# Another order for the set-up of a decoder layer kernel: which engine prepares what, and when

## The chip, the cores and the metric

The kernel runs on one core of a Trainium2 chip. A time is the device time of one execution in microseconds. The five engines of the core are TensorE (PE), VectorE (DVE), ScalarE (ACT), GpSimd (POOL) and SyncE (SP). Each runs its own list of instructions in order and waits for the others by semaphores; SP here only issues DMAs, and ACT and POOL issue some too.

## The reference

One decoder layer over x of shape (32, 128, 128): 32 batches of 128 tokens with 128 features. All in float32.

```
x = x + attn(layernorm(x))            # 16 heads of 8, rotary factors on q and k, causal softmax, W_attn, W_proj
x = x + xattn(ctx, ctx, layernorm(x)) # one head of 128, Wq, Wk, Wv, Wo, full softmax over 128 context rows
x = x + ffn(layernorm(x))             # router softmax over 8 experts, the top 2 of them, each silu(x Wg) * (x Wu) Wd,
                                      # plus a shared expert times sigmoid(x gate_w)
```

## The kernel before, in words

**Stages.** A batch is one tile of 128 tokens; four batches are a group (`GB`), eight groups in all. The kernel has a set-up, a loop over the 32 batches for both attentions and the router, then the passage to the experts and the expert part. The change lies in the set-up and in the first steps of the loop.

**Set-up.** SP and ACT issue the loads. PE turns W_attn, W_proj, Wo and the router weights (`transpose` against an identity), multiplies Wk with Wq and Wv with Wo so that each is one matrix later, spreads the rotary table over 128 rows and adds up two bias rows (L626 to L646). All of this goes to four shared PSUM banks, and DVE copies it to SBUF (L1108 to L1124). Before that DVE takes the statistics of the first group of x (L1084, L1089) and arranges the bias rows (`brow`, L1100). POOL writes constants, the causal masks and then normalises group 0 (L529, L531) and clears the value buffer (L561).

**First steps.** For a group, PE turns the normalised x (`turn_x`, L652), and projects keys and queries (`project`, L661: two matmuls of 512 columns); DVE adds the bias and multiplies with the rotary factors (L1146); DMAs put the heads into block form in `k_heads` and `q_heads` (L469), which must be zero elsewhere: that is what the clears of `wide` are for (L1096, 2048 columns each, one for each of keys and queries of two groups). For a batch, `project_v` (L668) makes the values, ACT drains them (L944), `scores` (L678) and a mask (L685) fill four PSUM banks, DVE takes row maxima (L1167), two of them by way of a copy by ACT (L951), `turn_max` (L694) turns them, ACT keeps them, a DMA spreads them (L475), and `scores_t` (L703 to L712) computes the transposed scores less the maxima, of which ACT takes the exponential (L955).

**Order.** Each engine's list in the loop comes from the table `ORDER`: entry (stage, offset, part, which) puts a stage of batch s + offset in slot s. The table is the same in both programs. On PE it yields `turn_x(0)`, `project(0)`, values 0 and 1, `scores(0)`, values 2, `turn_x(1)`, `turn_max(0)`, `scores(1)`, `scores_t(0)`, values 3, `project(1)`, and so on.

```
def late_setup():                      # DVE, L1128: ends_acc, kcol, ramp32, split of the shared expert's gate/up weights
setup_done                             # DVE tells it after the last copy (L1126); PE's project(0) and POOL's bias wait for it
```

## Time and profile before

| | us |
|---|---|
| median of 3 runs | 478.93 |
| lowest, highest | 478.83, 479.94 |
| profiled execution: its own time | 475.0 |
| profiled execution: span | 473.1 |
| PE busy | 427.4 (90%) |
| DVE busy | 358.2 (76%) |
| ACT busy | 293.0 (62%) |
| POOL busy | 203.5 (43%) |

The profiled execution is one of its own; its time stands beside the runs' and not among them. The span is what its instructions cover. Busy times are sums over the whole span and do not say who waits for whom at the start; the chain of waits and the timelines do. Names in the rows: `ps_scores` are the four PSUM banks of the scores, `ps_shared` the four others, `wide` the memory of `k_heads` and `q_heads`, `probs` also holds the raw weights during set-up. A row with xN merges N like instructions; a float32 matmul counts as two. The line numbers are those of the kernel before.

### The profile page before, as it was taken

To read this page: it belongs to the slowest core of one execution; us is meant where nothing else is said; L and a number is where in the kernel's file an instruction comes from. 1 tells how busy PE (TensorE), PEld (TensorE's weight loads), DVE (VectorE), ACT (ScalarE), POOL (GpSimd) and SP (SyncE) were. 2 spreads that over 40 slices of the span, in tenths; PEclk is the share of its full clock that TensorE was granted. 3 is DMA by queue.
4 is the path that set the end of the run, shared out by engine and by line. 5 is a ranking of instruction groups with operands and counts; after the bars stand their busy time and mean duration, and the time that the engine had idled before them with its cause. 6 is when DMAs were issued, how large, how long until landed. Compare 5 with 4: busy or idle time off the path is not lost.

```text
span 473.1 us, 13582 instructions
## 1 busy us (share of the span) xinstructions
PE 427.4 (90%) x4444; PEld 289.8 (61%) x4444; DVE 358.2 (76%) x1232; ACT 293.0 (62%) x951; POOL 203.5 (43%) x247
## 2 busy tenths in 40 slices
PE   4869799999999999999999988769899999999992
PEld 3424455555655655656555555547688888888782
DVE  5474567879889888888797786779577777777595
ACT  1124678887877877878779877463355555555430
POOL 7802012030343262353324235567166666676490
PEclk9999999999999999999999999559999999999998
DMA  7700000101111111011111003512233333232394
GB/s 191 198 24 26 19 19 31 37 10 35 49 29 50 48 48 49 26 54 47 33 47 53 25 28 110 169 51 76 67 100 98 92 93 92 81 104 62 110 318 135
DMA packets 41604, 34.69 MB, mean 73 GB/s; under 512 B 6464, under 2 KB 36432, under 8 KB 41536
## 3 DMA queue, kind: packets, MB, share of 16 engines
q1 hardware_dynamic: 36478, 24.51, 18.4%
q0 software_dynamic: 4320, 8.99, 5.6%
q8 instruction: 37, 0.61, 0.6%
q10 hardware_dynamic: 738, 0.33, 0.3%
q14 instruction: 31, 0.25, 0.2%
HBM read 17.26 MB, written 12.09 MB: 62 GB/s over the span
## 4 chain that ended last, share of the span: by engine, by line
PE 71%; DVE 12%; issue 6%; ACT 4%; POOL 3%; DMA 2%; SPq 1%; DVEq 0%; ACTq 0%; POOLq 0%
PE ps_scores L860 10%; PE ps_scores L678 7%; PE ps_shared L877 7%; PE ps_shared L725 6%; PE ps_scores L707 6%; PE ps_shared L661 3%; PE ps_shared L868 3%; PE ps_scores L703 3%; PE ps_shared L776 3%; ACT probs L955 2%; PE ps_scores L712 2%; POOL xs L593 2%; PE ps_shared L782 2%; PE ps_shared L787 2%; PE ps_scores L852 2%
## 5 line engine op out<-in xcount | busy, mean ns | idle before, releaser
L611 POOL DMA_INDIRECT ys<-ctx_t,xload x71 | 69.1, 974 | 45.2 <-ACT ctx_t L1052 42.7
L955 ACT ACTIVATE probs<-ps_scores 128x512 f32<-128x512 f32 x128 | 69.8, 608 | 17.9 <-PE ps_scores L712 17.9
L599 POOL TENSOR_TENSOR x1b<-x,bias 128x128 f32<-128x128 f32 x32 | 14.4, 451 | 151.0 <-DVE x L1188 151.0
L593 POOL DMA_INDIRECT xs<-xrow,posu x64 | 66.5, 1039 | 26.3 <-issue 13.2
L860 PE MATMUL ps_scores<-wide,xe 128*128 x213 | 66.9, 422 | 0.0
L951 ACT ACTIVATE s_copy<-ps_scores 128x512 f32<-128x512 f32 x64 | 38.4, 604 | 18.7 <-PE ps_scores L685 18.5
L1372 DVE COPY probs<-ps_shared 128x256 f32<-128x256 f32 x71 | 30.2, 425 | 22.8 <-PE ps_shared L868 22.8
L1167 DVE TENSOR_REDUCE negmax<-ps_scores 128x4 f32<-128x512 f32 x64 | 41.1, 684 | 7.4 <-PE ps_scores L685 6.9
L877 PE MATMUL ps_shared<-wd,probs 128*128 x284 | 43.4, 275 | 0.1
L678 PE MATMUL ps_scores<-wide,qk 32*128 32x512 f32 x256 | 38.4, 671 | 3.3 <-ACT probs L955 3.1
L1042 ACT ACTIVATE xe<-ps_scores 128x128 fp32r<-128x128 f32 x71 | 19.7, 278 | 33.8 <-PE ps_scores L852 33.8
L1167 DVE TENSOR_REDUCE negmax<-s_copy 128x4 f32<-128x512 f32 x64 | 40.0, 667 | 0.0
L1047 ACT ACTIVATE vst<-ps_scores 128x256 f32<-128x256 f32 x71 | 27.3, 384 | 18.6 <-PE ps_scores L860 18.6
L877 PEld LDWEIGHTS ps_shared<-wd,probs 128*128 128x128 f32 x284 | 37.2, 191 | 0.3 <-issue 0.3
L860 PEld LDWEIGHTS ps_scores<-wide,xe 128*128 128x128 f32 x213 | 34.8, 190 | 3.0
L725 PE MATMUL ps_shared<-probs,vst 128*32 128x128 f32 x1024 | 34.6, 276 | 0.0
L707 PE MATMUL ps_scores<-wide,qk 32*128 32x512 f32 x256 | 34.0, 601 | 0.0
L1366 DVE SCALAR_TENSOR_TENSOR vst<-vst,xload,ps_scores 128x256 f32<-128x256 f32 x71 | 33.5, 472 | 0.7 <-ACT vst L1047 0.6
L725 PEld LDWEIGHTS ps_shared<-probs,vst 128*32 128x32 f32 x1024 | 26.0, 109 | 5.3 <-issue 4.7
L868 PE MATMUL ps_shared<-ident,vst 128*128 128x128 f32 x142 | 27.2, 273 | 0.6 <-DVE vst L1366 0.5
L868 PEld LDWEIGHTS ps_shared<-ident,vst 128*128 128x128 f32 x142 | 19.5, 140 | 11.1 <-DVE vst L1366 2.1
L1361 DVE TENSOR_TENSOR xe<-ps_scores,xe 128x128 fp32r<-128x128 f32 x71 | 20.7, 292 | 5.0 <-ACT xe L1042 1.5
(220 smaller groups left out, 1012.1 us busy)
## 6 DMA issues: line engine op xcount, KB each, us to landing
xload<-xs SPq DMA_DIRECT2D x71, 66.0 KB, 1.9
wide<-qk SPq DMA_DIRECT2D x64, 64.0 KB, 1.9
wide<-ys SPq DMA_DIRECT2D x8, 512.0 KB, 7.4
ctx_t<-in_ctx SPq DMA_DIRECT2D x32, 64.0 KB, 2.0
out_x<-res SPq DMA_DIRECT2D x8, 256.0 KB, 3.4
ys<-ctx_t,xload POOLq DMA_INDIRECT x71, 2.3
wd<-in_L_ffn_w_down SPq DMA_DIRECT2D x8, 128.0 KB, 3.4
xs<-xrow,posu POOLq DMA_INDIRECT x64, 2.4
```

Source lines behind the costliest of these rows:

```text
L593: pool.indirect_dma_start(out=xs, out_offset=bass.IndirectOffsetOnAxis(ap=posu[:, g % 2, k, u:u + 1], axis=0), in_=xrow[:, g % 2, k, u, :] ...
L611: pool.indirect_dma_start(out=ys, out_offset=bass.IndirectOffsetOnAxis(ap=xload_i[:, i % XL, C + 1:C + 2], axis=0), in_=ybuf[:, i % 4, :], ...
L678: pe.matmul(bank[j][:], qk[r, g % 2, 0, ts], k_heads[r, g % 2, :, ts], start=True, stop=True)
L707: pe.matmul(bank[j][:], qk[r, g % 2, 1, ts], q_heads[r, g % 2, :, ts], start=False, stop=True)
L725: mm = pe.matmul(bank[VW * i:VW * (i + 1), half * T:(half + 1) * T], v_pairs[:, b % 4, pair, r * VH:r * VH + VW], probs[:, b % 2, 2 * pair ...
L860: mm = pe.matmul(PS[i % 2][:], a[:, i % 4, :], m[:, bass.ds(e, 1), :].rearrange("p a f -> p (a f)"), start=(r == 0), stop=(r == 2))
L868: mm = pe.transpose(PM[2 + i % 2][:, f * 128:(f + 1) * 128], xh[:, i % 3, f * 128:(f + 1) * 128], ident[:])
L877: mm = pe.matmul(PM[i % 2][:, 0:C], xhT[:, i % 3, f * 128:(f + 1) * 128], wd[:, bass.ds(e, 1), f, :].rearrange("p a c -> p (a c)"), start= ...
L951: act.activation(s_copy[:, j - 2, :], SC[score_bank(("scores", b), j)][:], ACT.Copy).then_inc(copied, 1)
L955: act.activation(probs[:, b % 2, j * HJ:(j + 1) * HJ, :].rearrange("p a t -> p (a t)"), SC[score_bank(("scores_t", b), j)][:], ACT.Exp)\
L1167: dve.reduce_max(negmax[:, b % 2, j * HJ:(j + 1) * HJ], part.rearrange("p (i t) -> p i t", i=HJ), axis=AX.X, negate=True).then_inc(maxed, 1)
L1366: dve.scalar_tensor_tensor(out=xh[:, i % 3, :], in0=xsilu[:, i % 3, :], scalar=xload[:, i % XL, C:C + 1], in1=PS[i % 2][:, FF:2 * FF], op0 ...
```

## The change

- **Loads.** SP asks for W_attn, the q/k bias row and the rotary table right behind the first group of x, under a semaphore of their own (`first_in`), then for group 1 of x, the small bias columns and rows, and the rest of x. Context and shared-expert loads come behind the query heads of group 0, and the nine loads of the down weights go into the loop, one with each `turn_x2`. Two of the four DMAs that place group 0's keys are issued by ACT.
- **PE** turns W_attn and makes rotary rows and q/k bias in two score banks; the other weights are turned behind `project(0)`, multiplied behind `scores(0)`, and the bias rows are made behind `scores(1)`.
- **ACT** loads its activation table before it issues its weight loads, and drains the weights that DVE drained.
- **DVE** clears `k_heads` of group 0 first, normalises group 0 row by row, and runs `late_setup` at group 1's `turn_x` entry instead of group 0's.
- **POOL** clears `q_heads` of group 0 and both buffers of group 1, normalises from group 1 on, and adds the attention bias to groups 0 and 1 together, when the bias rows are there.

```diff
+            sp.dma_start(wa, W_attn.rearrange("(k p) c -> p k c", p=128)).then_inc(first_in, 16)
+            sp.dma_start(rows[:, 2:4, :], b_attn[0:2 * C].rearrange("(a k n) -> a k n", a=1, k=2)).then_inc(first_in, 16)
+            sp.dma_start(rope4[:], rope[0:HD // 2]).then_inc(first_in, 16)
+            sp.dma_start(res[:, GB:2 * GB, :], x[GB:2 * GB].rearrange("b t c -> t b c")).then_inc(x_in[1], 16)
...
+                if b < NE:
+                    sp.dma_start(wd[:, b, :, :], (w_down[b] if b < E else sw_down).rearrange("(k p) c -> p k c", p=128))\
+                        .then_inc(wd_in, 16)
...
-                for i in range(HJ):
+                for i in range(HJ // 2 if g == 0 and n == 0 else HJ):
                     sp.dma_start(heads[i:128:HJ, g % 2, i, :], qk[i:128:HJ, g % 2, 1 - n, :]).then_inc(placed[g % 2], 16)
+                if g == 0 and n == 1:
+                    for u in range(4):
+                        sp.dma_start(ctx_t[:, u, :], ctx_in[u]).then_inc(ctx_loaded[u], 16)
+                    for k, m in enumerate((sw_gate, sw_up)):
+                        sp.dma_start(wgs_raw[:, k * FF:(k + 1) * FF], m).then_inc(wgs_in, 16)
...
+            pool.memset(q_heads[:, 0], 0.0).then_inc(heads_cleared[0][1], 1)
...
-            norm_x_rows(0)
             const(pool.memset(vst[:], 0.0))
             const(pool.memset(v_parts[:, :, 0:3:2, HD:HD + 1], 1.0))
             assert consts[0] == CONSTS + STORES
             pool.memset(one_row4[:].bitcast(fp32), 1.0).then_inc(ones_set, 1)
             pool.wait_ge(ones_set, 1)
+            norm_x_rows(1)
+            pool.memset(k_heads[:, 1], 0.0).then_inc(heads_cleared[1][0], 1)
+            pool.memset(q_heads[:, 1], 0.0).then_inc(heads_cleared[1][1], 1)
...
+                if g > 1:
                     norm_x_rows(g)
+                w.ge(x_normed, g + 1)
+                if g == 1:
+                    pool.wait_ge(set_drained[3], 2)
+                    add_bias(0)
+                add_bias(g)
...
+            pe.wait_ge(first_in, 16 * FIRST_LOADS)
 
             for k in range(3):
...
+                mm = pe.transpose(SC[0][:, k * C:(k + 1) * C], wa[:, k, :], ident[:])
+            mm.then_inc(set_filled[0], 1)
             pe.wait_ge(arranged, 2)
+            pe.matmul(SC[1][:, 0:2 * C], rope_rows[:], rope4[:].rearrange("p k t -> p (k t)"), start=True, stop=True)
             for k in range(2):
...
+                mm = pe.matmul(SC[1][:, 2 * C + k:2 * C + k + 1], brow[:, k, :], one_row[:, 0:1], start=True, stop=True)
             mm.then_inc(set_filled[1], 1)
 
...
+            def turned_weights():
+                pe.wait_ge(w_in, 16 * W_LOADS)
+                pe.transpose(PM[1][:, 0:C], wsq[:, 4, :], ident[:])
+                pe.transpose(PM[1][:, C:2 * C], wsq[:, 0, :], ident[:])
+                pe.transpose(PM[1][:, 2 * C:2 * C + NE], wr[:], ident[0:NE, 0:NE])
+                pe.matmul(PM[1][:, 3 * C:3 * C + 1], wsq[:, 1, :], cols[:, 2:3], start=True, stop=True).then_inc(set_filled[2], 1)
+
+            def folded_weights():
+                pe.wait_ge(set_drained[2], 1)
+                pe.matmul(PM[3][:, 0:C], wsq[:, 3, :], wsq[:, 1, :], start=True, stop=True)
+                pe.matmul(PM[3][:, C:2 * C], wsq[:, 2, :], woT[:], start=True, stop=True).then_inc(set_filled[3], 1)
+
+            def folded_biases():
+                pe.wait_ge(arranged, 3)
+                pe.matmul(PM[3][:, 2 * C:3 * C], bcol[:, 0, :], wpT[:], start=True, stop=False)
+                pe.matmul(PM[3][:, 2 * C:3 * C], one_row[:], rows[:, 0, :], start=False, stop=True)
+                pe.matmul(PM[3][:, 3 * C:4 * C], bcol[:, 1, :], woT[:], start=True, stop=False)
+                pe.matmul(PM[3][:, 3 * C:4 * C], one_row[:], rows[:, 1, :], start=False, stop=True).then_inc(set_filled[3], 1)
...
+                    if g == 0:
+                        pe.wait_ge(rows_normed, u + 1)
...
+                if g == 0 and n == 1:
+                    turned_weights()
...
+                if b == 0:
+                    folded_weights()
+                if b == 1:
+                    folded_biases()
...
+            act.preload_act_table_set("natural_log_exp_and_others")
             for n, m in enumerate((W_proj, Wo, Wq, Wk, Wv)):
...
+                    first_weights()
+                if g == 1:
+                    first_keys()
+                    turned_weights()
+
+            def first_weights():
+                act.wait_ge(set_filled[0], 1)
+                for k in range(2):
+                    act.activation(wqk[:, k, :].rearrange("p (r d i) -> p r d i", r=NJ, i=HJ),
+                                   SC[0][:, k * C:(k + 1) * C].rearrange("p (r i d) -> p r d i", r=NJ, i=HJ), ACT.Copy)
+                act.activation(wvT[:], SC[0][:, 2 * C:3 * C], ACT.Copy).then_inc(set_drained[0], 1)
+
+            def first_keys():
+                w.bank_read(("project", 0, 0))
+                act.wait_ge(heads_cleared[0][0], 1)
+                for i in range(HJ // 2, HJ):
+                    act.dma_start(k_heads[i:128:HJ, 0, i, :], qk[i:128:HJ, 0, 1, :]).then_inc(k_placed[0], 16)
+
+            def turned_weights():
+                act.wait_ge(set_filled[2], 1)
+                act.activation(woT[:], PM[1][:, 0:C], ACT.Copy)
+                act.activation(wpT[:], PM[1][:, C:2 * C], ACT.Copy)
+                act.activation(wrT[:], PM[1][:, 2 * C:2 * C + NE], ACT.Copy)
+                act.activation(bqA[:], PM[1][:, 3 * C:3 * C + 1], ACT.Copy, scale=XSCALE).then_inc(set_drained[2], 1)
+
+            def folded_weights():
+                act.wait_ge(set_filled[3], 1)
+                act.activation(wA[:], PM[3][:, 0:C], ACT.Copy, scale=XSCALE)
+                act.activation(wM[:], PM[3][:, C:2 * C], ACT.Copy).then_inc(set_drained[3], 1)
+
+            def folded_biases():
+                act.wait_ge(set_filled[3], 2)
+                act.activation(bias1[:], PM[3][:, 2 * C:3 * C], ACT.Copy)
+                act.activation(bias2[:], PM[3][:, 3 * C:4 * C], ACT.Copy).then_inc(set_drained[3], 1)
...
+            dve.memset(k_heads[:, 0], 0.0).then_inc(heads_cleared[0][0], 1)
             dve.wait_ge(const_ready, FIRST_CONSTS)
...
+            group_stats(0)
+            dve.wait_ge(first_in, 16 * FIRST_LOADS)
+            dve.tensor_copy(brow[:].rearrange("a k (r d i) -> a k r d i", r=NJ, i=HJ),
+                            rows[:, 2:4, :].rearrange("a k (r i d) -> a k r d i", r=NJ, i=HJ)).then_inc(arranged, 1)
+            dve.wait_ge(x_rstd, 1)
+            for u in range(GB):
+                dve.tensor_scalar(xn1[:, u, :], res[:, u, :], mv1[:, u, 0:1], rs1[:, u:u + 1], ALU.subtract, ALU.mult)\
+                    .then_inc(rows_normed, 1)
+            dve.wait_ge(rows_normed, GB)
+            dve.memset(rsum[:], 0.0).then_inc(x_normed, 1)
             dve.wait_ge(set_filled[1], 1)
...
+            dve.tensor_copy(ropes[:].rearrange("p k t -> p (k t)"), SC[1][:, 0:2 * C])
+            dve.tensor_copy(bqk[:], SC[1][:, 2 * C:2 * C + 2]).then_inc(set_drained[1], 1)
+            dve.wait_ge(w_in, 16 * W_LOADS)
+            dve.tensor_copy(bcol, cols[:, 0:2].rearrange("p (k a) -> p k a", a=1).broadcast_to([C, 2, C])).then_inc(arranged, 1)
...
             def turn_x(g):
-                if g == 0:
-                    clear(q_heads[:, 0])
-                    clear(k_heads[:, 1])
-                    clear(q_heads[:, 1])
+                if g == 1:
                     late_setup()
```

How instructions move, as the order of each engine's list shows it. First PE, from the bias matmuls of the set-up to the first values and scores; before (L652 turns x, L661 projects, L668 makes values):

```order
L632 MATMUL ps_shared<-one_row,brow 128x1 x2
L635 MATMUL ps_shared<-probs 128x128
L636 MATMUL ps_shared<-cols,probs 128x1
L637 MATMUL ps_shared<-rope,rope_rows 128x256
L642 MATMUL ps_shared<-woT,probs 128x128
L643 MATMUL ps_shared<-wpT,probs 128x128
L644 MATMUL ps_shared<-rows,one_row 128x128
L645 MATMUL ps_shared<-woT,probs 128x128
L646 MATMUL ps_shared<-rows,one_row 128x128
L652 MATMUL ps_shared<-ident,xn 128x128 x4
L661 MATMUL ps_shared<-xT,wqk 128x512 x2
L668 MATMUL ps_shared<-wvT,xT 128x128 x2
```

And now (L666 turns x, L675 projects, L642 to L645 turn weights, L682 makes values, L695 the first scores):

```order
L632 MATMUL ps_scores<-ident,probs 128x128 x3
L635 MATMUL ps_scores<-rope,rope_rows 128x256
L637 MATMUL ps_scores<-one_row,brow 128x1 x2
L666 MATMUL ps_shared<-ident,xn 128x128 x4
L675 MATMUL ps_shared<-xT,wqk 128x512 x2
L642 MATMUL ps_shared<-ident,probs 128x128
L643 MATMUL ps_shared<-ident,probs 128x128
L644 MATMUL ps_shared<-ident,wr 128x9
L645 MATMUL ps_shared<-cols,probs 128x1
L682 MATMUL ps_shared<-wvT,xT 128x128 x2
L695 MATMUL ps_scores<-wide,qk 128x512 x4
```

The weight products and bias rows, six matmuls, no longer stand ahead of the turn of x; three weight turns and a one-column matmul stand between projection and values.

DVE, from the q/k evictions of group 0 to the first row maxima (`negmax`); before:

```order
L1146 SCALAR_TENSOR_TENSOR qk<-ps_shared,bqk,ropes 128x512 x2
L1096 MEMSET wide 128x2048 x3
L1130 MEMSET ends_acc 128x48
L1131 CAST kcol<-ids 128x1
L1132 CAST ramp<-ramps 128x32
L1134 CAST wgs_hi<-probs 128x512
L1135 TENSOR_TENSOR wgs_lo<-probs,wgs_hi 128x512
L1167 TENSOR_REDUCE negmax<-ps_scores 128x4 x2
L1167 TENSOR_REDUCE negmax<-s_copy 128x4 x2
```

And now, from the copy of the bias columns on (L1191 is the q/k eviction, L1209 the row maxima):

```order
L1170 COPY probs<-cols 128x256
L1142 BN_STATS st<-res 128x6 x4
L1147 BN_AGGR mv<-st 128x2 x4
L1191 SCALAR_TENSOR_TENSOR qk<-ps_shared,bqk,ropes 128x512 x2
L1209 TENSOR_REDUCE negmax<-ps_scores 128x4 x2
L1209 TENSOR_REDUCE negmax<-s_copy 128x4 x2
L1142 BN_STATS st<-res 128x6 x4
L1147 BN_AGGR mv<-st 128x2 x4
L1209 TENSOR_REDUCE negmax<-ps_scores 128x4 x2
L1209 TENSOR_REDUCE negmax<-s_copy 128x4 x2
```

Three clears and the late set-up have left the place between the q/k evictions and the first row maxima; the statistics of group 1 stand ahead of the evictions now.

PE, from the mask matmuls of `scores(1)` to `scores_t(0)` (L703 and L707; now L724 and L728); before:

```order
L685 MATMUL ps_scores<-causal,ident 32x512
L685 MATMUL ps_scores<-causal,ident 32x4x96
L685 MATMUL ps_scores<-causal,ident 32x4x64
L685 MATMUL ps_scores<-causal,ident 32x4x32
L703 MATMUL ps_scores<-max_row,one_row 128x512 x4
L707 MATMUL ps_scores<-wide,qk 128x512 x4
```

And now:

```order
L702 MATMUL ps_scores<-causal,ident 32x512
L702 MATMUL ps_scores<-causal,ident 32x4x96
L702 MATMUL ps_scores<-causal,ident 32x4x64
L702 MATMUL ps_scores<-causal,ident 32x4x32
L654 MATMUL ps_shared<-wpT,probs 128x128
L655 MATMUL ps_shared<-rows,one_row 128x128
L656 MATMUL ps_shared<-woT,probs 128x128
L657 MATMUL ps_shared<-rows,one_row 128x128
L724 MATMUL ps_scores<-max_row,one_row 128x512 x4
L728 MATMUL ps_scores<-wide,qk 128x512 x4
```

Four matmuls of the bias rows have come in between; two weight products came in the same way behind `scores(0)`.

## Rows read from the trace of the kernel before

**Rows 1.** the page, its first line, part 4 (chain) and one row of part 6 (DMA)

```profile
span 473.1 us, 13582 instructions
...
PE 71%; DVE 12%; issue 6%; ACT 4%; POOL 3%; DMA 2%; SPq 1%; DVEq 0%; ACTq 0%; POOLq 0%
...
wide<-qk SPq DMA_DIRECT2D x64, 64.0 KB, 1.9
```

**Rows 2.** chain of waits, 15 to 45 us: start, length, what

```profile
16.78 3.77 PE ps_shared L661 x4
...
25.98 1.76 DVE wide L1096
...
28.88 2.48 DVE negmax L1167 x4
...
31.50 0.37 PE ps_shared L694
```

**Rows 3.** ten-microsecond windows: busy time (count) of each engine, PE clock, DMA

```profile
30.00:40.00 10.00, 7.09 (x56) 2.73 (x57) 4.98 (x15) 2.40 (x6) 0.00 (x0) 1.00 0.01 2
```

**Rows 4.** timeline of DVE: start, length, what, [idle before]

```profile
3.83 0.87 DVE L1084 BATCH_NORM_STATS2 st<-res 128x6 f32<-128x128 f32 x4 [3.83 <-DMA res<-in_x]
4.74 0.38 DVE L1089 BATCH_NORM_AGGREGATE mv<-st 128x2 f32<-128x6 f32 x4
...
7.01 0.72 DVE L1100 COPY brow<-rows 1x256 f32<-1x256 f32 x1
...
18.86 0.75 DVE L1146 SCALAR_TENSOR_TENSOR qk<-ps_shared,bqk,ropes 128x512 f32<-128x512 f32 x1 [1.74 <-PE ps_shared L661]
```

**Rows 5.** timeline of PE

```profile
6.79 0.87 PE L626 MATMUL ps_shared<-ident,probs 128*128 128x128 f32 x3 [6.79 <-POOL causal L557]
...
8.40 1.01 PE L632 MATMUL ps_shared<-one_row,brow 1*128 1x1 f32 x4
...
10.29 1.21 PE L637 MATMUL ps_shared<-rope,rope_rows 4*128 4x256 f32 x2
...
12.20 0.64 PE L643 MATMUL ps_shared<-wpT,probs 128*128 128x128 f32 x2
...
14.93 1.11 PE L652 MATMUL ps_shared<-ident,xn 128*128 128x128 f32 x4
16.78 3.75 PE L661 MATMUL ps_shared<-xT,wqk 128*128 128x512 f32 x4 [0.73 <-ACT xT L937]
...
22.54 0.79 PE L668 MATMUL ps_shared<-wvT,xT 128*128 128x128 f32 x2 [0.37 <-ACT vst L944]
23.40 2.09 PE L678 MATMUL ps_scores<-wide,qk 32*128 32x512 f32 x8
...
25.99 0.80 PE L668 MATMUL ps_shared<-wvT,xT 128*128 128x128 f32 x2
27.51 1.12 PE L652 MATMUL ps_shared<-ident,xn 128*128 128x128 f32 x4 [0.72 <-ACT vst L944]
...
31.80 2.09 PE L678 MATMUL ps_scores<-wide,qk 32*128 32x512 f32 x8
...
35.87 0.80 PE L703 MATMUL ps_scores<-max_row,one_row 1*128 1x512 f32 x4 [1.41 <-DVE negmax L1167]
...
39.48 2.09 PE L661 MATMUL ps_shared<-xT,wqk 128*128 128x512 f32 x4
```

**Rows 6.** timeline of DVE, in the loop

```profile
56.15 0.35 DVE L1198 TENSOR_SCALAR xn<-x,mv,rs 128x128 f32<-128x128 f32 x1 [1.02 <-ACT rs L973]
```

**Rows 7.** timeline of ACT

```profile
4.07 1.28 ACT L918 ACT_TABLE_LOAD   x1 [4.07 <-issue]
...
22.21 0.28 ACT L944 ACTIVATE vst<-ps_shared 128x128 f32<-128x128 f32 x1 [4.51 <-PE ps_shared L668]
```

**Rows 8.** timeline of POOL

```profile
13.87 0.21 POOL L562 MEMSET vst<- 128x64 f32 x1
```

**Rows 9.** timeline of the SP queue

```profile
11.85 4.02 SPq L448 DMA_DIRECT2D wd<-in_L_ffn_w_down  x8
```

More of the change, by code:

```diff
@@ L390, in bank_free @@
                 bank, first, width = SLOT[slot]
[L391 to L392 removed]
+                if n == 0 and bank in LATE_SETS:
+                    self.ge(set_drained[bank], LATE_SETS[bank])
                 self.ge(drained[slot], n)
```

111 lines of the change are left out of this document (28 added, 83 removed).

## The prediction

> **What bounds the kernel now.** I read four views, in this order. The page first [rows 1]: TensorE (PE) holds 71% of the chain that ended last, DVE 12%, everything else little. This change does not touch the main loop's work, so what counts is how early the loop gets under way. Next the chain of waits over 15 to 45 us [rows 2]: PE projects keys and queries, and then the chain leaves PE for DVE: three clears of the head buffers and the small late set-up, and only at 28.88 us the first row maxima, with PE's first turn of the maxima at 31.50. Then a window [rows 3]: PE is busy 7.09 of 10 us in 30 to 40. Last the timelines of DVE, PE, ACT, POOL and the SP queue [rows 4 to 9], for durations and spacings. My anchor is PE's first `scores_t(0)` matmul, at 35.87 us [rows 5]: everything that the change inserts or moves on PE lies ahead of it, and from there on both programs run the same instructions on PE in the same order.
>
> **The sum.** I follow the new path, with spacings of the old rows.
>
> Start. The first group of x lands at 3.83, its statistics end at 4.74+0.38 = 5.12 [rows 4]. The new program asks for W_attn, the q/k bias row and the rotary table right behind x, so I take them as landed by then. `brow` costs 0.72 [rows 4]: 5.84. PE, in program order, must do the rotary matmul (1.21) and the two bias matmuls (1.01) before it may turn x [rows 5]: 8.06. DVE's own normalising hides here: four 128x128 rows at 0.35 each, 1.4 [rows 6], behind ACT's rstd. ACT now loads its table (1.28, [rows 7]) ahead of its seven weight loads instead of behind; the statistics wait for either, so the order costs nothing unless ACT is free only after 8.06-1.4 = 6.7. From the first turn of x to the first projection it was 16.78-14.93 = 1.85 [rows 5]: projection at 9.91 instead of 16.78.
>
> To the first scores. The pair of projections takes 3.75: 13.66. Behind it PE now has three weight turns and a one-column matmul: 0.87, and half of 1.01: 15.03. ACT drains them in four copies, about 0.28 each as a like ACT row [rows 7]: 16.15. This wait is new, and behind it on ACT stands the drain of values 0, for which PE waits before values 1. From that drain to PE's next matmul was 22.54-22.21 = 0.33, and from there to the scores 0.86 [rows 5, 7]: `scores(0)` at 17.34 instead of 23.40. Two other inputs come earlier: the keys (DVE reads the projection 2.08 after it starts, 0.75 long [rows 4], then about 0.6 of issue on each of two queues and the 1.9 to landing of [rows 1], 15.3), and POOL's clear of the value buffer (14.08 [rows 8], less the two normalising operations now on DVE, plus one clear of 1.8 that came in: about 13.8).
>
> To the second scores. Scores and causal mask take 25.99-23.40 = 2.59: 19.93. The two weight products inserted here take half of the 2.73 that four such matmuls took (12.20 to 14.93): 21.30. Values 2 and its drain, 0.80+0.33: 22.43. Turning group 1, 1.12, and the maxima, 0.37 [rows 2, 5]: `scores(1)` at 23.92 instead of 31.80. DVE is no longer the one waited for: with the clears gone to POOL its row maxima start when the scores are there, about 19.7, and last 2.48 [rows 2], to 22.2.
>
> To the anchor. Scores and mask again 2.59: 26.51; the four bias matmuls inserted here 2.73: 29.24. In the old program PE waited 1.41 for DVE at this very place [rows 5], so about half of these matmuls is free and half is a loss. `scores_t(0)` comes at 29.2 instead of 35.87: **6.7 us earlier**, all of it at the slow pace of PE. In these sums I used whole durations where neighbours overlap slightly, and left x landing at its old time although ACT's loads no longer crowd it; I put 0.3 us back for that.
>
> **The clock.** The rows of PE run at two speeds. The two projections of group 0 take 3.75, the same pair of group 1 takes 2.09 [rows 5]; the slow ones go with the level of 1.2 GHz, the fast with 2.4, and the column of the granted clock, 1.00 in both [rows 3], does not show it. The change of level fell near 39.7 us, with PE without a gap since 35.87. A first stretch as free of gaps, 6.79 to 16.0, had not brought it. In the new program the gap of 1.41 is filled, so the stretch starts with `scores(1)` or before. If the rise comes as long into it as it did, PE is fast from about 27.5: the rest of the bias matmuls saves 0.7, and `scores_t(0)` with values 3, 39.48-35.87 = 3.61, shrinks in the ratio of 2.09 to 3.75 to 2.0: together 2.3. If it comes only behind `scores_t(0)`, as before, it saves nothing. I take 1.0. Total 6.7+0.3+1.0 = 8.0.
>
> On this the Trainium skill ("TensorE: Matmul & The Clock Gate", section "What's actually happening") says that the throttled state is the default and that activity releases it. By that alone the first stretch should have released it; this trace has it slow at 16.78, and the measurement decides. The rule would let the clock rise with the first scores already; that is a rival below, priced from rows.
>
> The skill ("ScalarE: Activation LUTs", "What ACT_TABLE_LOAD costs") adds a drain of about 1.38 us to each table load. Ahead of the weight loads that would hold all seven back; here the next ACTIVATE starts with the load's end, so I leave it out. With it, the answer would be some 0.7 later.
>
> **What I cost at nothing.** The nine loads of the down weights leave the front of the SP queue and are issued one per batch in the loop, 4.02/8 = 0.50 each [rows 9], where SP waits for the batch anyway. The late set-up (some 1.14: from the end of the last clear, 25.98+1.76, to 28.88 [rows 2]) moves behind group 1's place in the loop, where DVE stood idle 1.02 us for ACT [rows 6]. POOL's two further clears, 1.8 each, end by about 20, and keys of group 1 are wanted only behind its projection, some 8 us before 39.48 [rows 5]. The bias is added to two groups at once, 2.5 us of POOL behind 29.8, wanted only for batch 0's attention output, whose normalised row DVE made at 56.15 [rows 6]. Without that cover the loop pays the first two: at most 9 x 0.50 + 1.14 = 5.6.
>
> **The time.** The profiled execution has a span of 473.1 and a time of 475.0; less 8.0 it is 467.0. The median of the runs is 478.93, 3.9 above it; the difference lies around the span and in the run, and I carry it over: **470.9 us**.
>
> **Rivals.**
> 1. The clock rises early, during or just after `scores(0)`. For: PE's work from there on is dense. Against: the first stretch. `scores_t(0)` then waits for DVE again, as in the old program, where it began 35.87-31.80 = 4.07 after `scores(1)`: 23.92+4.07 = 28.0, 1.25 under the sum; behind it the 1.6 are saved, and some 0.4 on the turns ahead: 3.2. Gain 6.7+0.3+3.2 = 10.2: 468.7.
> 2. The work taken out of the set-up is paid in the loop: a down-weight load stands in front of the heads or the row maxima on SP, and the late set-up pushes row maxima. For: exactly these transfers gate `scores_t`. Against: SP's idle time. Half of 5.6 is paid, and the clock gives nothing: 478.93-7.0+2.8 = 474.7.
> 3. Slower: the clock comes late. PE's order is now another, with more small matmuls; if the change of level misses the stretch around `scores_t(0)`, everything behind stays slow, and each microsecond of work there costs one more. It decides when the slow stage lasts 8 us of fast work (16 us) beyond 29: a rise later than 45 us. A rise at 50 gives about 481. Against: in the old program the loop's density brought it at the first go.
> 4. The change does nothing for the loop: something unseen, a landing of W_attn or a constant of POOL, holds the first projection where it was. Only the DVE clears would then pay, and the bias matmuls eat them: within 1.4 us of 478.9.
>
> **Chances.** Forecast (469.5 to 472.5) 0.50; rival 1 0.20; rival 2 and lesser losses 0.21; rival 3 0.05; rival 4 0.04. Below 0.3% (1.4 us) a change can't be told from none. Faster 0.91, same 0.04, slower 0.05. The range runs from 467.2 (rival 1, and x landing earlier by some 0.6, and 0.9 for what the phase of the clock does at the passage to the experts) to 476.0 (rival 2 with most of its price).
>
> **What would show it.** Right: first projection near 9.9, `scores(0)` near 17, `scores(1)` near 24, `scores_t(0)` near 29 us; row maxima released by PE and not by the end of DVE's clears; bias matmuls directly ahead of `scores_t(0)`. The clock: whether the 3.61 of `scores_t(0)` with values 3 have become 2.0. Wrong: `scores(0)` after 19 (then a wait for POOL, the keys or ACT names itself); a step between two batches above the old one in the first nine batches (rival 2); slow matmuls after 45 us (rival 3).

## The result

The changed kernel takes 465.46 us (median of 4 runs, 464.1 to 467.28), the kernel before 478.88 us beside it: a ratio of 0.9729, 95% interval 0.9704 to 0.9755. It is 13.4 us faster; 8.0 were forecast, and the time lies below the range's low end of 467.2. The profiled execution, one of the four, took 466.55 us, with a span of 464.4, where that of before took 475.0 with 473.1. Of the runs below, one of `clears_back_keep` (496.82 us) and one of `fill_dip` (526.09) were slow executions, over 1.5% above the fastest of the same kernel, and count in no ratio and no median.

The page of the changed kernel, its first line and lines of its parts 1, 2 and 4, answers [rows 1] (here and below, lines that lie between those shown are left out):

```profile
span 464.4 us, 13583 instructions
PE 422.3 (91%) x4444; PEld 287.7 (62%) x4444; DVE 352.8 (76%) x1222; ACT 294.6 (63%) x962; POOL 209.3 (45%) x248
PEclk9998999999999999999999999588899999999997
PE 75%; DVE 9%; issue 6%; ACT 4%; POOL 3%; DMA 1%; SPq 1%; DVEq 0%; ACTq 0%; POOLq 0%
```

PE's share of the last chain rose from 71% to 75%, DVE's fell from 12% to 9%: PE waits less for DVE. PE's timeline of the first 38 us answers [rows 5] (columns: start, us, engine, line, operation, idle time before and its releaser):

```profile
5.05 0.87 PE L632 MATMUL ps_scores<-ident,probs 128*128 128x128 f32 x3 [5.05 <-DMA rope<-in_rotary]
7.65 1.12 PE L666 MATMUL ps_shared<-ident,xn 128*128 128x128 f32 x4
9.45 3.78 PE L675 MATMUL ps_shared<-xT,wqk 128*128 128x512 f32 x4 [0.69 <-ACT xT L993]
13.03 0.42 PE L642 MATMUL ps_shared<-ident,probs 128*128 128x128 f32 x1
14.24 0.77 PE L682 MATMUL ps_shared<-wvT,xT 128*128 128x128 f32 x2
15.38 0.79 PE L682 MATMUL ps_shared<-wvT,xT 128*128 128x128 f32 x2 [0.37 <-ACT vst L1000]
16.10 2.09 PE L695 MATMUL ps_scores<-wide,qk 32*128 32x512 f32 x8
18.70 0.53 PE L649 MATMUL ps_shared<-probs 128*128 128x128 f32 x2
21.41 0.27 PE L715 MATMUL ps_shared<-ident,negmax 128*16 128x128 f32 x1 [0.20 <-DVE negmax L1209]
21.61 1.14 PE L695 MATMUL ps_scores<-wide,qk 32*128 32x512 f32 x8
23.04 0.49 PE L654 MATMUL ps_shared<-wpT,probs 128*128 128x128 f32 x2
24.52 0.50 PE L724 MATMUL ps_scores<-max_row,one_row 1*128 1x512 f32 x4
28.71 1.14 PE L695 MATMUL ps_scores<-wide,qk 32*128 32x512 f32 x8
35.63 1.91 PE L695 MATMUL ps_scores<-wide,qk 32*128 32x512 f32 x8 [1.54 <-ACT probs L1013]
```

`scores(0)` (L695 at 16.10) still takes 2.09, the slow pace; `scores(1)` at 21.61 takes 1.14. So the level rose from 1.2 to 2.4 GHz near 18.9 (two float32 matmuls of 128 columns take 0.53 at 18.70, between the slow 0.80 and the fast 0.49), where it rose near 39.7 in the profile of before. `scores_t(0)`, the anchor (L724), starts at 24.52 instead of 35.87. `scores(3)` at 35.63 is slow again behind an idle 1.54; the window 35 to 40 has a granted clock of 0.66, that of before had 1.00. (The column does not show the slow stretch up to 18.9: it stands at 1.00 there.) DVE, answering [rows 2, 4]:

```profile
5.13 0.49 DVE L1158 COPY brow<-rows 1x256 f32<-1x256 f32 x1
5.82 1.61 DVE L1162 TENSOR_SCALAR xn<-res,mv,rs 128x128 f32<-128x128 f32 x4 [0.20 <-ACT rs L952]
18.79 1.29 DVE L1209 TENSOR_REDUCE negmax<-ps_scores 128x4 f32<-128x512 f32 x2 [4.77 <-PE ps_scores L702]
```

Its row maxima now wait 4.77 us for PE, not for its own clears. ACT drains the turned weights in four short copies from 14.41, then the values at 15.05, as forecast; its seven weight loads issue from 0.85 to 4.23 beside the table load of 0.82 to 2.10. Read one after another, PE's milestones give the whole account:

| start on PE, us | before | forecast | after | ahead |
|---|---|---|---|---|
| first projection | 16.78 | 9.91 | 9.45 | 7.33 |
| `scores(0)` | 23.40 | 17.34 | 16.10 | 7.30 |
| `scores(1)` | 31.80 | 23.92 | 21.61 | 10.19 |
| `scores_t(0)` | 35.87 | 29.2 | 24.52 | 11.35 |
| `scores(2)` | 41.77 | | 28.71 | 13.06 |
| `scores(4)` | 55.65 | | 43.86 | 11.79 |
| `scores(31)` | 272.78 | | 260.98 | 11.80 |
| end of the span | 473.1 | | 464.4 | 8.7 |

From `scores(4)` to `scores(31)` the two programs keep the same step to 0.02 us. The loads of the down weights and the late set-up, moved into this loop, cost nothing. Three things are to be explained: why the lead of the loop is 11.8 and not 8.0, why 3.1 of it is gone at the end of the span, and why the medians differ by 13.4 all the same.

### The profile page after: what moved, and what is told of

Same layout as the page of the kernel before. It is cut to its first block, busy times and chain, and to the rows that moved or that the text cites. A ratio compares the mean times of both kernels' runs of the same rounds, so it can differ in the third digit from the quotient of the medians.

```text
span 464.4 us, 13583 instructions
## 1 busy us (share of the span) xinstructions
PE 422.3 (91%) x4444; PEld 287.7 (62%) x4444; DVE 352.8 (76%) x1222; ACT 294.6 (63%) x962; POOL 209.3 (45%) x248
## 4 chain that ended last, share of the span: by engine, by line
PE 75%; DVE 9%; issue 6%; ACT 4%; POOL 3%; DMA 1%; SPq 1%; DVEq 0%; ACTq 0%; POOLq 0%
PE ps_scores L881 11%; PE ps_scores L695 8%; PE ps_shared L898 7%; PE ps_shared L746 7%; PE ps_scores L728 6%; PE ps_shared L675 4%; PE ps_shared L889 3%; PE ps_scores L724 3%; PE ps_shared L797 3%; POOL xs L599 3%; ACT probs L1013 2%; PE ps_scores L733 2%; PE ps_shared L803 2%; PE ps_shared L808 2%; PE ps_scores L873 2%
## 5 line engine op out<-in xcount | busy, mean ns | idle before, releaser
L599 POOL DMA_INDIRECT xs<-xrow,posu x64 | 68.5, 1070 | 25.7 <-issue 13.5
L881 PE MATMUL ps_scores<-wide,xe 128*128 x213 | 68.8, 433 | 0.0
L1209 DVE TENSOR_REDUCE negmax<-ps_scores 128x4 f32<-128x512 f32 x64 | 41.1, 684 | 11.8 <-PE ps_scores L702 11.2
L695 PE MATMUL ps_scores<-wide,qk 32*128 32x512 f32 x256 | 38.2, 668 | 3.2 <-ACT probs L1013 3.1
L1209 DVE TENSOR_REDUCE negmax<-s_copy 128x4 f32<-128x512 f32 x64 | 40.0, 666 | 0.0
L881 PEld LDWEIGHTS ps_scores<-wide,xe 128*128 128x128 f32 x213 | 35.9, 196 | 3.4 <-issue 0.2
L728 PE MATMUL ps_scores<-wide,qk 32*128 32x512 f32 x256 | 33.1, 586 | 0.0
```

Of the source, the lines that this page charges most:

```text
L599: pool.indirect_dma_start(out=xs, out_offset=bass.IndirectOffsetOnAxis(ap=posu[:, g % 2, k, u:u + 1], axis=0), in_=xrow[:, g % 2, k, u, :] ...
L695: pe.matmul(bank[j][:], qk[r, g % 2, 0, ts], k_heads[r, g % 2, :, ts], start=True, stop=True)
L728: pe.matmul(bank[j][:], qk[r, g % 2, 1, ts], q_heads[r, g % 2, :, ts], start=False, stop=True)
L881: mm = pe.matmul(PS[i % 2][:], a[:, i % 4, :], m[:, bass.ds(e, 1), :].rearrange("p a f -> p (a f)"), start=(r == 0), stop=(r == 2))
L1209: dve.reduce_max(negmax[:, b % 2, j * HJ:(j + 1) * HJ], part.rearrange("p (i t) -> p i t", i=HJ), axis=AX.X, negate=True).then_inc(maxed, 1)
```

## The experiments

The runs were on four chips. On one of them before takes 479 us as here (`after_third`, `fill_dip`, `warm_dip`, `clears_only`), on the three others about 500, so each time is compared only with runs of before on its own chip. The four profiles of before, of which three are from chips at 500, reach `scores(4)` at 55.65 to 56.67 us, so milestones of the first 60 us may be set side by side to about 1 us. My theory was that the mechanism is as forecast and the clock term too small. The milestones below are starts of `scores(b)`.

**The same kernels again.** They show how far executions of one program differ.

> The changed kernel once more, unchanged. My theory: the loop's start is fixed by waits and comes again to 0.1 us (scores of batch 2 at 28.7, the last scores at 261, 11.8 earlier than in the old profile), and the 3 us that single executions differ by arise in one place, the passage from the loop to the experts (270 to 330 us), and in where TensorE's clock changes level. Rival: the executions differ already at the start of the loop by a us or more, so that 11.8 is itself a matter of luck. Time 464 to 467.

> The kernel before once more, unchanged. Its profiled execution (475.0) was 3.9 under the median of its runs. My theory: that execution was a lucky one in the passage to the experts or in the clock at the start, and a second profile has the last scores at 272.8 again but a span of 474 to 477. Rival: 3.9 is a constant between a profiled execution and the others; then this profile gives 475.0 again while its runs stay at 479.

> The changed kernel again, for comparison on the same chip. Both theories: 0.972 to 0.980 of the time of the kernel before, scores(0) near 16.2 us, a slow scores(3) and a step of 8.2 us to scores(4), where the other batches take 6.95.

`before_again`: ratio 1.0018 (0.9994 to 1.0042). `after_again`: 0.9791 (0.9749 to 0.9833). `after_third`: 0.9709 (0.9672 to 0.9747), 464.4 us, just under the expected 0.972 to 0.980. The expected clock did not hold, nor did "to 0.1 us": `after_again` has `scores(2)` at 27.70 and not 28.7, `scores(4)` at 42.84, which is 13.6 ahead of `before_again` on the same chip. The profile of `before_again` took 504.49, 1.4 over the median of its runs, so 3.9 under it is not a constant of profiled executions. It has on PE:

```profile
23.47 1.14 PE L678 MATMUL ps_scores<-wide,qk 32*128 32x512 f32 x8 [0.69 <-DMA wide<-qk]
31.57 0.37 PE L694 MATMUL ps_shared<-ident,negmax 128*16 128x128 f32 x1 [4.49 <-DVE negmax L1167]
31.87 2.09 PE L678 MATMUL ps_scores<-wide,qk 32*128 32x512 f32 x8
```

The old kernel too can be fast at `scores(0)`; it then falls back in the wait of 4.49 behind DVE's clears. The same fall shows in `before_third`, and in `before_fourth`, which is fast from 26.8 on: in all three the granted clock is 0.50 in the window 35 to 40. The profile from which I predicted, slow all the way to 39.7, was the exception of four. `after_third` on PE:

```profile
12.23 1.06 PE L675 MATMUL ps_shared<-xT,wqk 128*128 128x512 f32 x1
13.09 0.34 PE L642 MATMUL ps_shared<-ident,probs 128*128 128x128 f32 x1
15.41 1.14 PE L695 MATMUL ps_scores<-wide,qk 32*128 32x512 f32 x8
33.78 1.14 PE L695 MATMUL ps_scores<-wide,qk 32*128 32x512 f32 x8 [1.54 <-ACT probs L1013]
```

Here the level is up from 13 us, and the same idle 1.54 ahead of `scores(3)` leaves it up: batch 4 starts at 40.74, 14.9 ahead of the profiled before, and not 11.8. So one instruction stream gives a lead of 11.8 to 14.9 at batch 4, and only the level of the clock differs.

**`clears_back`: the changed kernel with DVE's three clears back in their old place.**

```diff
 def turn_x(g):                                # DVE
+    if g == 0:
+        dve.memset(q_heads[:, 0], 0.0).then_inc(heads_cleared[0][1], 1)
+        dve.memset(k_heads[:, 1], 0.0).then_inc(heads_cleared[1][0], 1)
+        dve.memset(q_heads[:, 1], 0.0).then_inc(heads_cleared[1][1], 1)
```

The three POOL clears are left out in return.

> The changed kernel with three clears (query heads of group 0, both of group 1) back on DVE behind the query eviction of group 0. My theory: row maxima of batch 0 start at 20.8 instead of 18.8 and the second scores come 2.0 us later (23.6 instead of 21.6), the rest follows: 2 us slower, about 467.5, since DVE has 4.8 us of idle time there to take 6.4 us of clears. Rival: the clears were the bulk of the gain, as three of them with gaps held the chain 6.4 us in the old program; then 471 or more. Second rival: the longer gap on TensorE keeps the clock at its lower level through the second scores (2.09 instead of 1.14 each), and 3 to 5 us are lost.

Measured: 0.9889 (0.9854 to 0.9924), 497.02 against 490.51 us of `after_again` on the same chip: 6.5 us are lost, where my theory had 2. The size is that of the first rival, the slow second scores are those of the second. PE:

```profile
15.95 1.14 PE L692 MATMUL ps_scores<-wide,qk 32*128 32x512 f32 x8
23.50 0.37 PE L712 MATMUL ps_shared<-ident,negmax 128*16 128x128 f32 x1 [3.62 <-DVE negmax L1210]
23.81 2.09 PE L692 MATMUL ps_scores<-wide,qk 32*128 32x512 f32 x8
26.40 0.80 PE L651 MATMUL ps_shared<-wpT,probs 128*128 128x128 f32 x2
35.56 1.14 PE L692 MATMUL ps_scores<-wide,qk 32*128 32x512 f32 x8
```

The clears make PE idle for 3.62, and the window 25 to 30 has a granted clock of 0.50. `scores(1)` starts 3.2 later than in `after_again` (20.59), but it starts slow (2.09), and PE's work stays slow to some 34: `scores(2)` is 7.9 later (27.70), batch 4 6.6 (42.84). The second half could be the clock or something behind the clears, so the next kernel fills the gap.

**`clears_back_keep`: the same, with work for PE in its idle time** (eight matmuls whose result nobody reads, ahead of the first turn of the maxima).

```diff
 def turn_max(b):                              # PE
+    if b == 0:
+        for _ in range(8):
+            pe.matmul(PM[1][:, 256:512], ident[:], <ident, 256 columns>)
```

> As clears_back (three clears on DVE again), and eight further matmuls of 256 columns on TensorE (results not used, about 0.43 us each at the upper level) in the gap in which it waits for the row maxima of batch 0. Theory: of the 6.5 us that clears_back cost, about 3 are the wait itself and the rest is the clock that fell in the gap; with the gap filled the second scores take 1.14 each again, and it is 3 to 3.5 us slower than the changed kernel instead of 6.5 (scores of batch 2 near 31 in place of 35.6). Rival: the clock level follows time or chance and not TensorE's idle time; then it stays as clears_back, or worse by what the fillers delay.

Measured: 0.9753 (0.9708 to 0.9798). PE:

```profile
19.82 3.62 PE L711 MATMUL ps_shared<-ident 128*128 128x256 f32 x16
23.51 1.14 PE L692 MATMUL ps_scores<-wide,qk 32*128 32x512 f32 x8
30.62 1.14 PE L692 MATMUL ps_scores<-wide,qk 32*128 32x512 f32 x8
```

DVE is as late as in `clears_back`, `scores(1)` starts within 0.3 of it, and now runs fast: `scores(2)` comes at 30.62 instead of 35.56, only 2.9 later than in `after_again`. The clears in this program cost 2.9 of wait and 4.9 of clock up to `scores(2)`. The time of this run does not show the 2.9: its ratio is not above that of `after_again`, on another chip, whose profile lost 1.3 at `scores(3)`.

**`before_keep`: the old kernel with ten such matmuls in its gap.**

> The kernel before with ten such matmuls in its gap of 4.5 us ahead of the turn of the first maxima. Theory: the clock, already up at the first scores in the second profile of this kernel, stays up, so the second scores, scores_t(0) and the projections of group 1 run at the upper level: scores of batch 2 at 39.5 instead of 42.5, 3 us faster than before. Where the clock rose late (as in the first profile, 39.7) the fillers bring it up themselves and cost at most 1 us of delay. Rival: no change within 0.5 us.

Measured: 1.0001 (0.9961 to 1.0042). PE:

```profile
28.41 6.54 PE L693 MATMUL ps_shared<-ident 128*128 128x256 f32 x20
34.99 1.14 PE L678 MATMUL ps_scores<-wide,qk 32*128 32x512 f32 x8
```

A miss as an improvement: the level was low when the fillers began, so they took 6.54, from 28.41 on, where before turns its maxima at 31.50 [rows 2], and held up `scores(1)` by 3. The rise that came under them paid back part of it: `scores(4)` comes at 57.33, 0.7 to 1.7 behind the four profiles of before, and the time shows no difference within 0.4%. Filling a gap keeps a level that is up; where it is down, the filler is itself in the way.

**`clears_only` and `clears_behind`: the kernel before with the clears alone moved to POOL.** In the first they stand ahead of POOL's routing constants, in the second the two for group 1 stand behind them.

```diff
 pool.wait_ge(ones_set, 1)
+pool.memset(q_heads[:, 0], 0.0).then_inc(heads_cleared[0][1], 1)
+pool.memset(k_heads[:, 1], 0.0).then_inc(heads_cleared[1][0], 1)  # clears_only
+pool.memset(q_heads[:, 1], 0.0).then_inc(heads_cleared[1][1], 1)  # clears_only
...
 pool.iota(ramps[:], pattern=[[128, 32]], base=0, channel_multiplier=0).then_inc(const_ready, 1)
+pool.memset(k_heads[:, 1], 0.0).then_inc(heads_cleared[1][0], 1)  # clears_behind
+pool.memset(q_heads[:, 1], 0.0).then_inc(heads_cleared[1][1], 1)  # clears_behind
```

> The kernel before with one part of the change alone: the three clears behind the first turned x are made by POOL behind its value buffers, the rest is the old program. Theory (the clears cost a wait of 2.9 and, through the idle TensorE, its clock): scores(0) stays at 23.4, the row maxima start when the scores are there, scores(1) comes at 28.9 instead of 31.8, and scores(2) 6 to 8 us ahead of before: 1.2 to 1.6% faster in all. Rival (wait alone): 2.9 us at scores(1) and at scores(4), 0.6% faster. Second rival (POOL is late with the buffers and its later constants hold the late set-up): less than 1.5 us.

> clears_only with POOL's second and third clear behind its routing constants, so that DVE's late set-up need not wait for these. Theory (what clears_only lacked is this wait of 2.7 us on DVE): late set-up at 21.4, row maxima at 26.1 with the scores, scores(1) at 28.9, 2.9 ahead of before; at scores(4) 2.2 to 6 ahead, as the clock goes; 0.5 to 1.2% faster in all. Rival (the clears had cost nothing but idle time that is there anyway): 1.3 us ahead from scores(4) on, as in clears_only.

`clears_only`: 0.9956 (0.9938 to 0.9973), `scores(1)` 1.96 ahead of before, batch 4 1.27: less than the theory's 1.2 to 1.6%, and the second rival, in part. DVE in `clears_only`, then in `clears_behind`:

```profile
24.03 0.10 DVE L1130 MEMSET ends_acc<- 128x48 f32 x1 [2.70 <-POOL ramps L581]
26.93 1.27 DVE L1164 TENSOR_REDUCE negmax<-ps_scores 128x4 f32<-128x512 f32 x2
```

```profile
20.91 0.10 DVE L1130 MEMSET ends_acc<- 128x48 f32 x1
26.18 1.29 DVE L1164 TENSOR_REDUCE negmax<-ps_scores 128x4 f32<-128x512 f32 x2 [2.89 <-PE ps_scores L688]
```

The clears delayed POOL's constants, and DVE's late set-up waited 2.70 for them. Behind the constants they no longer hold it: the late set-up starts at 20.91, DVE waits for PE, `scores(1)` comes at 29.10 as expected (28.9), batch 4 2.1 to 2.4 ahead of the two profiles of before on that chip (`before_third`, `before_fourth`), and the time is 0.993 of before (0.9908 to 0.9951). The clears alone are thus worth 0.7%, the wait and no clock: `scores(0)`, `scores(1)` and `scores_t(0)` ran at the slow pace (2.09, 2.09, 0.80), although values 0 and 1, at 21.01 and 21.86, had been fast (0.49). The order of the set-up alone is `clears_back`, 1.1%. The product, 0.982, is near the 0.9791 of the whole.

**`fold_gap` and `warm_fold`: the four bias matmuls** moved ahead of `scores(3)` with their two ACT drains behind the maxima of batch 2; the second also has fillers ahead of the loads and of the first projection. In both the bias rows are formed from columns that exponentials have overwritten by then, so they are not the reference's; the work is the same.

```diff
 def scores(b):                                # PE
+    if b == 3:
+        folded_biases()
...
-    if b == 1:
-        folded_biases()
```

> The changed kernel with the four bias matmuls not behind scores(1) but ahead of scores(3), where TensorE is idle 1.5 us in every profile of the changed kernel and the clock then falls for 3 us (scores of batch 3 at 1.6 to 1.9 instead of 1.14, batch 4 comes 1.27 late); ACT drains them behind the maxima of batch 2. Theory: scores_t(0) starts when it did, within 0.2, since DVE's maxima gate it (so the four matmuls cost nothing now, not half of 2.73), the gap is filled, the clock stays up, and 1.3 us are won. Rival: the matmuls were in the way of scores_t(0), and their going saves another 1 us or more there. Second rival: the bias comes late for batch 0's attention output and the gain is lost.

> fold_gap, with three matmuls of 256 columns ahead of the first loads' wait and three in the wait for the first turned x. From the earlier test with two of 512 columns: the clock rose at 6.5 and fell again near 8.2 us, ahead of the projections. Theory: with the second gap filled too it stays up through the projections (2.1 for the pair, not 3.5 to 3.8), and the first scores come about 1.5 us earlier than in the changed kernel; with fold_gap together 2.5 to 3 us faster than it. Rival: the fillers end too late for the projection at the lower level and cost 0.5 us.

`fold_gap`: 0.9753 (0.9705 to 0.9801). `warm_fold`: 0.9749 (0.9708 to 0.9791); the intervals overlap those of the changed kernel, so the 1.3 and the 2.5 to 3 us that I expected are not there. PE in `warm_fold`:

```profile
21.51 1.14 PE L702 MATMUL ps_scores<-wide,qk 32*128 32x512 f32 x8
24.42 0.50 PE L729 MATMUL ps_scores<-max_row,one_row 1*128 1x512 f32 x4 [1.41 <-DVE negmax L1216]
```

From `scores(1)` to `scores_t(0)` it takes 2.91, just as with the matmuls between (21.61 to 24.52): at 2.4 GHz they take 1.48 and lie wholly in the 1.41 that PE otherwise waits for DVE, but for 0.07. PE in `fold_gap`:

```profile
22.65 2.09 PE L697 MATMUL ps_scores<-wide,qk 32*128 32x512 f32 x8
26.72 0.80 PE L724 MATMUL ps_scores<-max_row,one_row 1*128 1x512 f32 x4 [1.41 <-DVE negmax L1211]
```

Here the level rose only near 31, and `scores(2)` came at 33.41, 4.7 behind the changed kernel's profile. That is a third place for the rise, in a program that is the same up to `scores(1)`. At the slow pace the way from `scores(1)` to `scores_t(0)` takes 4.07 without the four matmuls and 4.77 with them (`clears_back`).

**`warm_start`, `fill_dip`, `warm_dip`: fillers in the changed kernel.** `warm_start` has two float32 matmuls of 512 columns ahead of the wait for the first loads; `fill_dip` three of 256 columns ahead of `scores(3)`; `warm_dip` both.

```diff
 pe.wait_ge(const_ready, FIRST_CONSTS)
+for _ in range(2):
+    pe.matmul(SC[2][:], ident[:], <ident, 512 columns>)   # warm_start, warm_dip
 pe.wait_ge(first_in, 16 * FIRST_LOADS)
...
 def scores(b):                                # PE
+    if b == 3:
+        pe.wait_ge(set_drained[3], 2)
+        for _ in range(3):
+            pe.matmul(PM[3][:, 0:256], ident[:], <ident, 256 columns>)   # fill_dip, warm_dip
```

> The changed kernel with two further float32 matmuls of 512 columns (results not used) on TensorE while it waits for the first loads, from 2.0 to about 5.4 us. Theory of the clock: the dense stretch raises the clock before the projections, whose pair then takes 2.1 instead of 3.8, and the first scores come about 2 us earlier, at 14: about 463. Rival: the clock does not rise on it, or falls again in the gaps up to 9.4 us; then nothing moves but up to 0.3 us lost to the last of the two matmuls.

> The changed kernel with three 256-column matmuls, whose result nobody reads, in the idle 1.5 us of TensorE ahead of scores(3). Theory (the idle time drops the clock and that alone makes batch 3 slow): scores(3) takes 1.14 and not 1.64 to 1.91, the step to scores(4) is 6.95 and not 8.2, and all from there on is 1.27 us earlier, 0.3% of the time. Rival (the level falls at this place whatever fills the gap, or the fillers run slow and push scores(3) back): the same step of 8.2 or more, 0 to 1.5 us later than the changed kernel.

> fill_dip with two 512-column float32 matmuls ahead of the first weights too (at 2.0 to 5.8 us). Theory: the clock is up from scores(0) on, which gave 1.3 us there, and stays up: 1.3+1.27 = 2.6 us ahead of the changed kernel, 0.994 of its time. Rival (the level of the first 15 us is settled anew by later gaps, and the gain seen before was an accident of one execution): only the 1.27 of fill_dip, or nothing.

`warm_start`: 0.9753 (0.9716 to 0.9789), 488.84 against 490.51 of `after_again`, whose interval it meets. `fill_dip`: 0.9681 (0.9657 to 0.9705), 464.44 over the three runs that count. `warm_dip`: 0.9669 (0.965 to 0.9688), 463.23, against 464.4 of `after_third`. PE in `warm_start`, then in `fill_dip`:

```profile
2.00 3.78 PE L630 MATMUL ps_scores<-ident 128*128 128x512 f32 x4 [2.00 <-POOL one_row L546]
7.07 0.50 PE L639 MATMUL ps_scores<-one_row,brow 1*128 1x1 f32 x4
9.37 3.45 PE L677 MATMUL ps_shared<-xT,wqk 128*128 128x512 f32 x4 [0.69 <-ACT xT L995]
```

```profile
34.34 1.46 PE L689 MATMUL ps_shared<-ident 128*128 128x256 f32 x6
36.04 1.14 PE L699 MATMUL ps_scores<-wide,qk 32*128 32x512 f32 x8 [0.24 <-ACT probs L1017]
```

The early fillers bring the level up by 7 us; it falls again somewhere in PE's idle times of 0.17 and 0.69 before 9.37, where three of the four matmuls of the projection take 1.06 each, as in the slow profiles, and `scores(0)` starts at 14.98, 1.3 ahead of `after_again`. The later fillers fit the gap, and the step to batch 4 is 6.96. But `after_third` has the same step without them, so this pays only in executions that would have dipped, and no gain over the changed kernel is measured. `warm_dip` is the fastest on its chip by its median, by 1.2 us; its interval meets that of `after_third`, so it is not shown to be faster.

**The passage to the experts.** Of the lead of 11.8, 3.1 are gone by the end.

> The kernel before again, one look. Theory (the profiled execution that the prediction used was a short one at the passage to the experts, 270 to 335 us, by about 3 us): here from scores(31) to the end it takes 3 us more than there, like the changed kernels, the span is 475 to 477. Rival (the change itself costs 3 us at the passage): the same 200 us from scores(31) to the end as in the first profile, a span of 473.

> As before_third; by the theory both have the longer passage, by the rival neither.

From `scores(31)` to the end of the span it takes 200.3 us in the profiled before, but 203.4 in the changed kernel, 203.7 in `after_third`, 203.2 in `fill_dip`, 202.9 in `warm_dip`, and 203.4 in `clears_only`, whose program is the old one there. The two further profiles of before are from another chip; there it takes 216.4 and 218.9 (`clears_behind` 219.6), so the spans and the bound of 3 us that they were to be held against can't be applied, but one unchanged program varies by 2.5 us in this part. On the chip of `after_again` it takes 222.6 in the changed kernel and 223.4 in `before_again`, so the change costs nothing here. The first place where the longer executions fall behind is POOL's scatter of the last rows. POOL and PE in before, in the changed kernel and in `clears_only`:

```profile
326.07 1.38 POOL L593 DMA_INDIRECT xs<-xrow,posu  x1 [0.30 <-issue]
333.45 0.33 PE L852 MATMUL ps_scores<-ident,xload 128*128 128x128 f32 x1 [1.13 <-DMA xload<-xs]
```

```profile
314.15 3.65 POOL L599 DMA_INDIRECT xs<-xrow,posu  x1 [0.30 <-issue]
323.13 0.47 PE L873 MATMUL ps_scores<-ident,xload 128*128 128x128 f32 x1 [2.87 <-DMA xload<-xs]
```

```profile
324.67 3.66 POOL L596 DMA_INDIRECT xs<-xrow,posu  x1 [0.30 <-issue]
333.79 0.48 PE L855 MATMUL ps_scores<-ident,xload 128*128 128x128 f32 x1 [3.00 <-DMA xload<-xs]
```

One scatter takes 2.3 us longer, PE then waits 1.7 longer for the rows, and comes out of the wait at the slow pace (0.47 and 0.48 against 0.33). At this first matmul the two are 1.5 behind, and within the next 7 us, in which PE's rows are slow, 3.0. Since `clears_only` has it too, the change of the set-up's order is not needed for it. The two profiles of the unchanged kernel on one chip, `before_third` and `before_fourth`, differ in the same scatter:

```profile
331.51 1.39 POOL L593 DMA_INDIRECT xs<-xrow,posu  x1 [0.31 <-issue]
331.15 3.66 POOL L593 DMA_INDIRECT xs<-xrow,posu  x1 [0.31 <-issue]
```

The first of them waits 1.12 for the rows and is the shorter by 2.5 us from `scores(31)` on. The short scatter is in these two profiles, before and `before_third`, and in none of the fifteen others, of either program, where PE waits 2.8 to 3.1. So the profiled before was a short execution: 475.0 against its median of 478.9, and 3.1 of these 3.9 us lie in the passage. What makes a scatter take 3.65 was not found.

## Why the prediction missed

**The mechanism held.** Every wait was where the prediction put it: weights turned ahead of `scores(0)`, ACT's four copies in front of the values, row maxima released by PE, bias matmuls directly ahead of `scores_t(0)`. Nothing is paid in the loop, so rival 2 is refuted by the table; so are rivals 3 and 4. Rival 1 had the clock right, and its 468.7 was nearer, but not its reason for stopping: at the fast pace `scores_t(0)` begins 2.91 after `scores(1)` and not 4.07, and the bias matmuls just filled PE's wait for DVE.

**"In these sums I used whole durations where neighbours overlap slightly ... I put 0.3 us back."** This term was too small. Up to `scores(0)`, slow in both programs, the answer was 1.24 us earlier than the sum: the first turn of x at 7.65 and not 8.06, the pair of projections 3.58 from start to next start and not 3.75, four ACT copies 0.64 and not 1.12 (two of them, of 9 columns and of 1, are also smaller than the row that priced them). From there to `scores_t(0)` the same kind of error can be read from executions at 1.2 GHz: `scores(0)` to `scores(1)` takes 5.87 in `fold_gap` against 6.58 in the sum, `scores(1)` to `scores_t(0)` 4.77 in `clears_back` against 5.28. Together 1.24+0.71+0.51 = 2.46, where I had put 0.3. This takes the slow pace from other executions, so it is a reading across runs.

**"I take 1.0" for the clock.** Too small as well. Against these the profiled execution gains 5.87-5.51 = 0.36 and 4.77-2.91 = 1.86 ahead of the anchor. Behind it, `scores_t(0)` to `scores(2)` takes 4.19 instead of 5.90: 1.71. The dip at `scores(3)` takes 1.27 back (its step to batch 4 is 8.23; 6.96 without a dip). In sum 2.66; without the dip, 3.9. I had argued from one execution where the rise comes; the profiles of the changed set-up without early fillers have it between 13 and 31 us, and three of the four profiles of before have a first rise ahead of 27, lost again in the wait for the clears. 6.7+2.46+2.66 = 11.8, the lead of the loop.

**"About half of these matmuls is free and half is a loss."** At the slow pace the loss is 4.77-4.07 = 0.70, about half of the 2.73-1.41 = 1.32 in the sum (part of the 0.51 above). At the fast one it is nothing (`warm_fold`).

**"The difference lies around the span and in the run, and I carry it over."** To carry it was right, the reason half wrong. 3.1 of the 3.9 us are the short passage of that one profile, which neither the change nor the medians share. Profile against profile therefore shows only 8.45 us, close to my 8.0 by accident: the 3.8 missed above and the 3.1 of the passage nearly cancel. Set right for the passage, the profiled before would take 475.0+3.1 = 478.1, 0.8 under its median, and the profiled after stands 1.1 over its own; 8.45+3.1+0.8+1.1 gives the 13.4, as it must, since 0.8 and 1.1 are what is left over. These 1.9 I can only argue: the profiled after had the dip and a rise at 18.9, and `after_third`, without the dip and up from 13 us, was 3.1 further ahead, so the usual execution may lie between the two.

On the clock, `after_third` was fast from 13 us, the profiled run from 18.9, `fold_gap` from 31. The Trainium skill ("TensorE: Matmul & The Clock Gate", "What's actually happening") has activity release the throttle; the trace agrees that the rise comes under work and that a filled gap keeps it (`clears_back_keep`), but the place of the rise does not follow from the instruction stream alone. The 0.7 at the table load that the prediction left out did not appear: the first projection came before the sum's time, and the weight loads were issued beside the table load.

What stays open: what sets the place of the rise in one execution, and why an idle 1.54 ahead of `scores(3)` makes it slow in only some; why a single scatter takes 1.4 or 3.65 us; and what the two parts of the change would give on a chip where before takes 479, since `clears_back` ran only on another.

## What to carry to other kernels

In these runs an idle time of PE costs its length and, if the level falls with it, up to half of the time that PE's work then takes until the next rise: here 2.9 and 4.9 us. So price an early wait by both, and look at a PE row that occurs every batch (here `scores`, 2.09 or 1.14) to see which level holds. Where a profile is 4 us off its median, look for the stage that holds the difference, by comparing a part that the change can't touch; two profiles alone would have told of 8.45 us where the medians tell of 13.4. When clears go to another engine, look at what is queued behind them there: in front of POOL's constants they led by 1.3 us at batch 4, behind them by 2.1 to 2.4.

## What the hardware showed that I had not expected

- A rise and a fall within 7 us: fillers from 2.0 brought PE up by 7.07 (bias matmuls 0.50 instead of 0.85), and the projection at 9.37 was slow again.
- With the same idle 1.54 us ahead of it, `scores(3)` of the changed kernel took 1.91 in one execution, 1.64 in a second and 1.14 in a third. Of all thirteen profiles with this idle time, of either kernel, three have it slow (the third is `warm_start`, 1.87).
- A table load of 1.28 us on ACT ran while ACT's queue issued DMAs at 0.25 to 0.58 each, as in before (0.23 to 0.58).
- Indirect scatters of one form mostly take 0.97 us on POOL; two of them take 2.99 to 3.67 at the same place in fifteen of the seventeen profiles, and the second of these 1.38 and 1.39 in the other two.
- The granted clock of a window can stand at 1.00 over a stretch at the slow pace (up to 18.9 in the changed kernel), and at 0.50 over another (35 to 40 in `before_again`): the length of a repeated row tells the pace.
